# The q and k stacks take another road: from on-chip part buffers through a scratch array in HBM

## The reference

```python
h = jnp.maximum(_layernorm(x, axis=-1), 0.0)
q, k, v = heads(h @ Wq + bq), heads(h @ Wk + bk), heads(h @ Wv + bv)   # 16 heads of 32
scores = jnp.einsum('bhqd,bhkd->bhqk', q, k) * scale
scores = jnp.where(mask[:, None] == 0, -jnp.inf, scores)
attn = jax.nn.softmax(scores, axis=-1)
out = jnp.einsum('bhqk,bhkd->bhqd', attn, v)
return x + out.transpose(0, 2, 1, 3).reshape(b, s, D_MODEL) @ Wo + bo
```

## Time and profile before

| | |
|---|---|
| time, median of 3 runs | 1643.15 us (1640.05 to 1648.43) |
| the profiled execution | 1643.36 us, its span 1641.5 us |
| PE / PEld busy | 1587.1 us (97%) / 1024.8 us (62%) |
| DVE / ACT busy | 1439.5 us (88%) / 1425.8 us (87%) |
| POOL busy | 746.8 us (45%) |
| SP's queue in DMA time | 40.7% of 16 engines, 180.23 MB |
| HBM read / written | 54.79 MB / 16.78 MB |

### The profile page before, as it was taken

How to read it: one execution, slowest core, us unless ns; L and a number is a source line. 1 busy time by engine, 2 the same in 40 slices (tenths; PEclk the granted TensorE clock), 3 DMA queues, 4 the chain that set the end, 5 groups by cost and what they waited for, 6 DMA issues and landing times.

```text
span 1641.5 us, 27359 instructions
## 1 busy us (share of the span) xinstructions
PE 1587.1 (97%) x7489; PEld 1024.8 (62%) x7489; DVE 1439.5 (88%) x3504; ACT 1425.8 (87%) x3436; POOL 746.8 (45%) x673
## 2 busy tenths in 40 slices
PE   6799999999999999999999999999999999999987
PEld 5546666666666666666666666666666666666643
DVE  5888889898898989889898899989989898888886
ACT  3689898889989899898989989889898988989984
POOL 3044444454454544444454454544544554553542
PEclk9789999999999999999999999999999999999999
DMA  6434443444434444443444434344443544434320
GB/s 211 101 95 116 113 119 87 142 106 119 117 93 133 102 128 110 118 111 88 142 104 121 118 89 140 95 130 110 115 121 82 143 100 122 122 93 109 95 85 27
DMA packets 154032, 183.56 MB, mean 112 GB/s; under 512 B 67724, under 2 KB 69784, under 8 KB 153880
## 3 DMA queue, kind: packets, MB, share of 16 engines
q1 hardware_dynamic: 149400, 180.23, 40.7%
q10 hardware_dynamic: 4480, 1.58, 0.4%
HBM read 54.79 MB, written 16.78 MB: 44 GB/s over the span
## 4 chain that ended last, share of the span: by engine, by line
PE 68%; DVE 14%; SPq 7%; issue 5%; ACT 4%; DMA 2%; DVEq 0%; ACTq 0%
PE psP L772 30%; PE ps L829 14%; PE psO L859 11%; PE ps L841 10%; SPq L234 5%; DVE ps L625 4%; ACT ps L469 3%; DVE probs L639 2%; SPq L274 2%; PE ps L786 1%; DVE probs L642 1%; DVE part_lo L680 1%; DVE neg_max L625 1%; DMA q_stack<-part_hi 1%; DVE stats L537 1%
## 5 line engine op out<-in xcount | busy, mean ns | idle before, releaser
L374 POOL TENSOR_TENSOR probs<-probs,keep_k 128x512 int32<-128x512 int32 x438 | 574.3, 1332 | 608.4 <-ACT probs L509 606.4
L625 DVE CUSTOM_DVE_ANT_0 ps<-ps,bias_q 128x512 f32<-128x512 f32 x1024 | 707.6, 692 | 156.0 <-PE ps L829 151.0
L469 ACT ACTIVATE ps<-ps,neg_max 128x512 f32<-128x512 f32 x1024 | 686.0, 670 | 138.5 <-DVE neg_max L625 111.8
L509 ACT ACTIVATE probs<-ps 128x512 f32<-128x512 f32 x1024 | 617.5, 604 | 13.5 <-PE ps L841 11.4
L829 PE MATMUL ps<-k_stack,q_stack 96*128 96x512 f32 x1024 | 450.1, 440 | 24.1 <-ACT ps L469 17.5
L841 PE MATMUL ps<-q_stack,k_stack 98*128 98x512 f32 x1024 | 412.9, 404 | 4.9 <-ACT probs L509 3.7
L829 PEld LDWEIGHTS ps<-k_stack,q_stack 96*128 96x128 f32 x1024 | 194.6, 190 | 284.1 <-ACT ps L469 166.3
L639 DVE SCALAR_TENSOR_TENSOR probs<-turned,probs 128x512 f32<-128x512 bf16 x512 | 358.3, 701 | 2.1 <-ACT probs L509 2.1
L859 PE MATMUL psO<-probs,v_sb 128*32 128x512 f32 x2048 | 275.3, 610 | 8.5 <-DVE oT_lo L655 3.3
L841 PEld LDWEIGHTS ps<-q_stack,k_stack 98*128 98x128 f32 x1024 | 196.6, 192 | 47.1 <-ACT probs L509 16.1
L469 ACT ACTIVATION_READ_ACCUMULATOR ps<-ps,neg_max 128x1 f32 x1024 | 215.0, 210 | 0.0
(11 more groups left out here) (76 smaller groups left out, 1908.4 us busy)
## 6 DMA issues: line engine op xcount, KB each, us to landing
q_stack<-part_hi SPq DMA_DIRECT2D x512, 64.0 KB, 2.0
k_stack<-part_hi SPq DMA_DIRECT2D x504, 64.0 KB, 2.0
x_tile<-in_x_dram SPq DMA_DIRECT2D x66, 256.0 KB, 3.0
turned<-in_adj_dram SPq DMA_DIRECT2D x64, 256.0 KB, 3.0
q_stack<-part_lo SPq DMA_DIRECT2D x256, 64.0 KB, 2.0
k_stack<-part_lo SPq DMA_DIRECT2D x256, 64.0 KB, 2.0
y_tile<-in_x_dram SPq DMA_DIRECT2D x62, 256.0 KB, 2.9
out_dram<-y_tile SPq DMA_DIRECT2D x62, 256.0 KB, 2.1
```

The lines of the kernel that those rows point to most:

```text
L374: nc.gpsimd.tensor_tensor(bits, bits, keep_k[:, kt // 2, :], ALU.mult).then_inc(gpsimd_masked, 1)
L469: nc.scalar.activation(item, item, ACT.Exp, scale=-1.0, bias=neg_max[:, g % 2, col:col + 1], accum_out=exp_sum[:, col:col + 1]).then_inc(e ...
L509: nc.scalar.activation(probs[:, n % P_RING, :], ps2[:, n % 2, :], ACT.Exp, scale=SCALE).then_inc(exp2_done, 1)
L625: nc.vector.tensor_tensor_reduce(bank1(k, ("s", u)), bank1(k, ("s", u)), bias_q[:, qt, :], -SCALE, 3.0e38, ALU.add, ALU.min, neg_max[:, g ...
```

## The change

The parts of a tile no longer go straight into the stack. A scratch array `part_rows` of 2 x 4 x 128 x 512 floats lies in HBM. `store_parts` writes `part_hi` and `part_lo` of a tile there in two transfers of 256 KB; `load_stack` reads three times 256 KB back, one for each row of the stack with its four heads at once, after waiting until the stores have landed. All five are on SP's queue, the stores at the slot where ACT and DVE are due to have written the parts (u % 4 == 1) and the loads two slots later. ACT no longer issues any of them. The last tile of a block is stored at slot 1 and loaded at slot 3 of the next block. ACT and DVE now wait for the store of tile i - 2 (`hi_out`, `lo_out`) where they waited for the stack. PE's waits stand where they stood, with other counts.

```diff
+        part_rows = nc.dram_tensor("part_rows", [2, 4, P, S], F32).ap()
-        def load_stack(queue, b, i, pieces=("hi0", "lo", "hi1")):
...
-                for j in range(GROUP):
-                    queue.dma_start(stack[row:row + 32, g, j, :].bitcast(F32),
-                                    part[32 * j:32 * j + 32, i % 2, :].bitcast(F32)).then_inc(stack_in[kind], 16)
+            def store_parts(b, i):
+
+                kind, g = QK_ORDER[i]
+                sp.wait_ge(stack_in[kind], due(48 * (4 * b + g - 1)))
+                sp.wait_ge(qk_hi_done, 8 * b + i + 1)
+                sp.dma_start(part_rows[0, i % 4], part_hi[:, i % 2, :].bitcast(F32)).then_inc(hi_out[i % 2], 16)
+                sp.wait_ge(qk_lo_done, 8 * b + i + 1)
+                sp.dma_start(part_rows[1, i % 4], part_lo[:, i % 2, :].bitcast(F32)).then_inc(lo_out[i % 2], 16)
+
+            def load_stack(b, i):
+
+                kind, g = QK_ORDER[i]
+                stack = q_stack if kind == "q" else k_stack
+                lo_row = 64 if kind == "q" else 32
+                sp.wait_ge(scores2, due(64 * (b - 1) + 16 * (g + 1)))
+                sp.wait_ge(stack_in[kind], 48 * (4 * b + g))
+                sp.wait_ge(hi_out[i % 2], part_stored(b, i))
+                for row in (0, 32, 64):
+                    if row == lo_row:
+                        sp.wait_ge(lo_out[i % 2], part_stored(b, i))
+                    sp.dma_start(stack[row:row + 32, g].bitcast(F32),
+                                 part_rows[int(row == lo_row), i % 4].rearrange("(j d) s -> d j s", d=DH)).then_inc(stack_in[kind], 16)
...
-                    if u in (8, 10, 12) and have(k - 1):
-                        load_stack(sp, k - 1, 7, (("hi0",), ("lo",), ("hi1",))[(u - 8) // 2])
-                    if u % 4 == 1 and u > 1:
-                        done = tile_at(k, u // 4 - 1)
-                        if done and done[0] in "qk" and done != ("k", 0, 0):
-                            load_stack(sp, done[2], QK_ORDER.index(done[:2]))
-                        if done == ("k", 0, 0):
-                            load_stack(sp, 0, QK_ORDER.index(("k", 0)), ("lo",))
+                    done = tile_at(k, u // 4 - 1) if u >= 4 else tile_at(k - 1, 15)
+                    if u % 4 == 1 and done and done[0] in "qk":
+                        store_parts(done[2], QK_ORDER.index(done[:2]))
+                    if u % 4 == 3 and done and done[0] in "qk":
+                        load_stack(done[2], QK_ORDER.index(done[:2]))
...
-                            wait_stack_loaded(*((b, i - 2) if i >= 2 else (b - 1, i + 6)))
+                            act.wait_ge(hi_out[i % 2], part_stored(b, i - 2))
...
-                            wait_stack_loaded(*((b, i - 2) if i >= 2 else (b - 1, i + 6)))
+                            dve.wait_ge(lo_out[i % 2], part_stored(b, i - 2))
...
-                            pe.wait_ge(stack_in["q"], due(192 * (4 * b + g + 1)))
-                            pe.wait_ge(stack_in["k"], due(192 * (4 * b + g + 1)))
+                            pe.wait_ge(stack_in["q"], due(48 * (4 * b + g + 1)))
+                            pe.wait_ge(stack_in["k"], due(48 * (4 * b + g + 1)))
```

More of the change, by code:

```diff
@@ L136, in attention_block @@
         stack_in = {"q": sem("q_stack_in"), "k": sem("k_stack_in")}
+        hi_out, lo_out = [sem("hi_out0"), sem("hi_out1")], [sem("lo_out0"), sem("lo_out1")]
         c_in = sem("c_in")
@@ L213, in vector_before, with part_stored @@
             return max(n, 0) - gpsimd_counts[max(n, 0)]
-        def load_stack(queue, b, i, pieces=("hi0", "lo", "hi1")):
[L217 to L232, removed]
-                for j in range(GROUP):
-                    queue.dma_start(stack[row:row + 32, g, j, :].bitcast(F32),
-                                    part[32 * j:32 * j + 32, i % 2, :].bitcast(F32)).then_inc(stack_in[kind], 16)
+        def part_stored(b, i):
+            return 16 * (4 * b + i // 2 + 1)
         def halves(b, g):
@@ L415, in _ @@
         def _(act):
[L416 to L420, removed]
             def load_c(b, g):
@@ L489, in step @@
                             act.wait_ge(qkv_done, due(qkv_before(b, kind, n) + 1))
-                            wait_stack_loaded(*((b, i - 2) if i >= 2 else (b - 1, i + 6)))
+                            act.wait_ge(hi_out[i % 2], part_stored(b, i - 2))
                             bias = (bq_col if kind == "q" else bk_col)[:, n:n + 1]
                             nc.scalar.activation(part_hi[:, i % 2, :], psP[:, T % 2, :], ACT.Identity, bias=bias).then_inc(qk_hi_done, 1)
-                            if (kind, n, b) == ("k", 0, 0):
-                                load_stack(act, 0, QK_ORDER.index(("k", 0)), ("hi0",))
                         elif kind == "v" and not (b > 0 and n >= 2):
@@ L499, in step @@
                             nc.scalar.activation(v_sb[:, (4 * b + n) % 6, :], psP[:, T % 2, :], ACT.Identity).then_inc(v_done, 1)
-                            if (n, b) == (3, 0):
-                                load_stack(act, 0, QK_ORDER.index(("k", 0)), ("hi1",))
                     b, n = pass2(k, u)
@@ L525, in _ @@
         def _(dve):
-            def wait_stack_loaded(k, i):
-                kind, n = QK_ORDER[i]
-                if have(k):
-                    dve.wait_ge(stack_in[kind], due(192 * (4 * k + n + 1)))
             def ln_stats(b, t):
```

## The result

The changed kernel takes 1656.76 us (median of 7 runs, 1654.15 to 1659.27) against 1643.15 of before (7 runs beside it, 1639.2 to 1650.07): ratio 1.0077, 95% interval 1.0055 to 1.0099. It is slower, by more than the 0.5% that can be told from nothing. The prediction, 1639 with a range of 1630 to 1650, is wrong. The profiled execution took 1658.49 us, its span is 1656.6.

A forecast was written before the change was run, and what follows sets the result against it. The prediction took PE to bound the steady blocks and SP the start. From 1643.36 us it took 3 for the start and 1.5 for the first block's mask, 0 elsewhere: 1638.9, say 1639, range 1630 to 1650.

The forecast's parts named there:

- Part 1: SP's queue: the change gives SP some 20 us a block back, worth nothing in the steady part.
- Part 2: Round trip of k0's stack through HBM: slack before slot 35 grows from 3.0 to 6.2 us; the wait costs nothing.
- Part 3: DMA engines: 4.2 MB more a block, share from 0.42 to 0.54 to 0.58; nothing saturates, price 0.
- Rival 2: ACT's small constants land late behind the stack bursts, in two groups a block: slower, 1661 us; chance 0.09.
- Part 4: Start of the kernel, where SP bounds: mask and k0 come earlier, gain 2.2 to 4.1 us, taken as 3.
- Part 5: First block: second mask turn some 8 us earlier, gain 0 to about 4 us, taken as 1.5.
- Rival 4: Start: PE's clock falls elsewhere and takes 3 to 4 us again, so 1643 us; chance 0.17.

The follow-up runs named there:

- e3: The kernel before with only the k1 tile sent through HBM, the other seven tiles direct as before: 1660.14 us, ratio 1.009.
- e7: The changed kernel with only the k1 tile sent directly between SBUF buffers as before: 1647.39 us, ratio 1.0015.
- e8: The changed kernel with k1's three loads held by a wait until PE has done the score of slot 42: 1648.5 us, ratio 1.0029.
- e5: The changed kernel with POOL's add to y at slot 15 held until DVE has done its masking of slot 13: 1654.98 us, ratio 1.0053.
- e12: The changed kernel with first q0 and k0 direct, POOL's add held as in e5, k1's loads held as in e8, first y load at slot 38: 1637.18 us.
- e1: The changed kernel with k1's three loads at slot 43 of SP's list in place of 39, without an added wait: 1658.87 us, ratio 1.008.

## Why the prediction was wrong, by its own steps

- **Part 1** (SP's time) was right on what SP's time is worth: SP left the chain and the steady blocks gained nothing. A load's issue took 0.32 to 0.37 us (median) where I took 0.55.
- **Part 2** (round trip) was right: the stacks cost PE 0.6 us in the whole run. The term "lands 3.0 us on" was mis-sized, 3.8 to 3.9 measured, without harm to the stacks: k0's last load lands 3.5 to 4.7 us ahead of slot 35, for 2.1 to 3.9 before and 6.2 forecast.
- **Part 3** is the step that failed: "Nothing saturates. Price 0". The share, 0.54, was forecast; but it is a mean. The row that it was divided by, 0.74 at 262 GB/s, has loads to 128 partitions; loads to 32 partitions fill the engines at about 225 GB/s (last section), so the three loads of a stack are 3.5 us of full engines, and ACT's constants stand behind them. Price measured: 16.7 us in interval 11.
- **Rival 2** described that mechanism: ACT's constants behind the bursts, deciding from a landing of 2.9 us. It got the sign right, the landing nearly (3.6; measured 4.1 to 4.3), and two groups of four where it was one. It had 0.09 because "the loads of 256 KB that pass now have given PE 0.9 us of such waits"; no row had four of them in a row. e3, e7 and e8 each show it.
- **Part 4** (start, -3) had the wrong sign: first group +3.9. "Stores 32.3 to 33.0, landed 35.1" took the 2.1 us that is the median of the output stores; they stood behind 1.05 MB, landed at 38.4 and 39.0, and SP went on at 38.4. "Landed and taken by DVE at 35.3" failed in the same way: 37.8. The passage of the Trainium skill that the prediction weighed ("SBUF — State Buffer", "Door 1: The DMA port swizzle") was nearer: it gives 218 GB/s at most for 32 neighbouring partitions, and the trace has 231 with full engines (last section), which is what counts. The prediction put its rate on k0's own loads alone, 1 to 2 us, and not on what waits behind q0's, nor on part 3. With the rate in all three places, 0.79 MB at 218 is 3.6 us of queue ahead of ACT's constants: an estimate from that page which passes rival 2's 2.9 us.
- **Part 5** was right that the second `keep_k` comes sooner: 79.82 for 84.48 (8 us forecast). The wait of 1.15 us for POOL is gone. But the first block is shorter by 3.1 us (1.5 taken, 0 to 4 given), and PE was at half clock for 10.3 us less of it; how much of the 3.1 is the mask's isn't shown, and that they lie in the range given is no proof of the step.
- **Rival 4** (the clock, 0.17) saw that the clock takes part here, but at the first block it gave: up to the end of that block PE was at half clock for 34.1 us before and 30.7 after, 6.8 more ahead of the first group and 10.3 less behind it.
- **Not foreseen** at all: y's earlier arrival, which lets POOL's add run beside DVE's multiply, 4.7 us in interval 4 (e5). "Users that are not waiting" can be users that start earlier.

The sum by the pieces of the table: 1643.4 + 3.9 - 3.1 + 16.9 - 2.6 = 1658.5, the profiled execution. It must come out, since the table splits the span; a cause that a run shows have only the 3.9 and, within the 16.9, intervals 4 and 11.

## What to carry to other kernels

A mean DMA share says nothing of a small transfer's wait: ask how many bytes stand in front of it at the moment it is issued, divided by the rate at which those bytes go to their partitions, and compare that with its slack. If it doesn't fit, hold the burst back on a semaphore behind the small transfer, and look at once what stands behind the burst on its own queue (e8, then e12); moving an issue to a later place in a list that runs ahead does nothing (e1). A cheaper queue paid nothing where PE was the bound, in the steady blocks. And before a gain at the start or the end is put down to a change, compare the granted clock of that stretch in both traces, and in a few traces of kernels that differ by nothing there.

## What the runs showed of the hardware that was not expected

- Loads from HBM to 32 partitions filled the 16 DMA engines at about 225 GB/s. Kernel after, a stretch with only three such loads, then one of the start in which a mask load and stores on 128 partitions were under way (share and GB/s last):

```profile
166.00:169.00 3.00, 2.59 (x12) 1.85 (x11) 2.90 (x8) 2.47 (x6) 0.00 (x0) 1.00 1.02 231
36.00:37.00 1.00, 1.00 (x6) 0.81 (x6) 0.00 (x0) 0.69 (x1) 0.00 (x0) 1.00 0.96 358
```

- An 8 KB transfer from ACT's queue that was issued behind 1.05 MB of SP's landed in 4.1 to 4.3 us, when nearly all of it had moved, against 1.8 in e8: it wasn't let past for being small or for coming from another engine. Its first packet ran 3.2 us after the issue, in e8 1.2 us. Over the blocks with the loss the middle one of the constants' data packets ran 2.5 to 3.9 us after the first issue, in the block at 740 1.9 us.
- A DVE multiply of 128x512 in bf16 and fp32 took 0.69 us alone. One that began inside a POOL add of 128x512 fp32 took as long as the add still had, and some 0.55 us: 1.29 (median of 14) with 0.74 us of the add left in the kernel after, 0.95 (median of 12) with 0.40 left before. Where the add began inside the multiply, the multiply kept its 0.69 and the add took 1.5 to 1.6 us for 1.3. It matters which of the two begins first.
- The way through HBM is not slow in itself: a 256 KB store lands in 2.1 to 2.2 us (median), as a 64 KB move from SBUF to SBUF did in 2.0. Behind 1.05 MB the same store took 6.4 us.
